# A gated cross-attention layer with a 4-bit FFN: where DVE decodes the weights, and when TensorE turns the FFN's tokens

## The chip, the cores and the metric

One core of one Trainium2 chip. The metric is the device time of one execution in microseconds, the median of the runs. Engines: PE (TensorE), with its weight loads as PEld; DVE (VectorE); ACT (ScalarE); POOL (GpSimd); SP (SyncE), which issues all the DMAs here.

## The reference

Sixteen sequences of 100 tokens, 512 wide. First a cross-attention with 16 heads of 32 onto a context of 361 rows with a mask, then an FFN whose weights are 4-bit codes with a scale for each group of 128:

```
x = x + tanh(g_xattn) * sigmoid(h @ wg.T) * (softmax(q k.T / sqrt(32), masked) v @ wo.T),   h = rmsnorm(layernorm(x)) * norm_w
gate, up = split(layernorm(x) @ dequant(gate_up).T)          # 2 x 1408 rows, 512 wide
y = (silu(gate) * up) @ dequant(down).T                       # 512 rows, 1408 wide
x = x + tanh(g_ffn) * y / sqrt(mean(y * y) + 1e-6)
```

dequant takes a nibble of a 32-bit word, looks it up in a table of 16 values (0 to 6, both signs) and multiplies it by its group's scale.

## The kernel before

Every matrix product in float32 is made of halves: a "hi" half, rounded by ACT, and a "lo" half, the rest, made by DVE (in places by POOL). Three matmuls (hi hi, hi lo, lo hi) make one product.

**Attention.** Four groups of four sequences. A group has 16 steps, one for each head. In step i, PE turns the probabilities of head i (L1364), attends with head i - 1 (L1377), makes the scores of the next four heads in steps 2, 6, 10 and 14 (L1346, L1353), and then does the one to three jobs that BESIDE lists for the step (L271): X (turn normalised tokens, L1315), Q, K, A/B (values), T (turn the heads' outputs), G (gate), O (output product). The jobs share two banks, PJ, in the order of CYCLE (L265), so that a job starts when the low half of the job two before it has been taken out (open_bank, L1287). Q0 also waits for the low half of X3, and each T for its four heads. Steps 11 to 15 already do the jobs of the next group. ACT in a step (L730): pT_hi, the exp of the head two steps ahead, the hi halves of the jobs, ctxT_hi. DVE in a step (L966): pT_lo, attention norm of the head before (reciprocal, o), the row maximum of the head two ahead (nmax), in steps 6 to 9 the statistics of a sequence of the next group, the low halves of the jobs and the outputs, and the normalising of a sequence. Each engine runs its list in order; what is queued behind a wait waits too. POOL makes rstd by a power, ctxT_lo in steps 9 to 11 and the mask bias.

**Decoding beside it.** The FFN's weights are decoded by DVE in the first three of the four groups. A loop body (L1203) goes from step LOOP_FROM = 6 to step 5 of the next group. Each body decodes six pieces, of kinds u, d, u, u, d, u (u: a gate/up tile; d: two down tiles with their scales). A piece goes through stages (decode, L1033): 0 shifts the words (a d piece also cuts its scales), 1 takes the magnitude (d: scale less its cut), 2 puts in the sign, 3 writes `left`, 4 (d alone) writes the second `left`. Piece q lies in step 8 + q, its five stages in five places of the step. SP (L480 to L516) loads the words of pieces 0 and 1 and the first scales at the start of the body (pieces_before), each further piece's when the piece two before it has been decoded, and stores each `left` (512 KB) to DRAM; `words` and `left` have two buffers each. SP's list of a body: pieces 0 to 3, then the loads of the group after (tokens when X has been made, context, mask), pieces 4 and 5, and then the four outputs.

**FFN.** Five groups j of 320 tokens, 11 tiles t of 128 hidden columns each. PE makes eight products into five banks taken in turn (L1526) and two or three chunks of the down product (L1539); ACT and DVE take each product out with its scale (L838, L1221); POOL adds the two halves; then come tanh, two DVE products (L1229 is called gated, L1236) and the halves of the hidden values. The next group's tokens are normalised by DVE in t = 3, 4 and 5 (L1097), turned by PE at the start of t = TURN_AT[m] into bank 1 (transpose_tile, L1410), which waits until mT_lo of the turn before has read that bank; mT_hi is ACT's and mT_lo (L1105) DVE's, at the end of that t.

Of the kernel before, what the change touches and what calls it, by code (L numbers as in the profile page):

```python
# [18 lines left out]
NB = 4  # L19
GROUPS = B // NB  # L20
# [8 lines left out]
STEPS = HEADS  # L29
# [23 lines left out]
KINDS = "uduudu"  # L53
# [7 lines left out]
def build(nc, x, ctx_tail, ctx_full, mask, mask_tail, g_xattn, g_ffn, norm_w, wq, wk, wv, wo, wg,  # L61
          packed, gu_scales, dn_scales, identity, shifts, x1_dram, gu_dram, dn_dram, out):
    es = ExitStack()
    with es:
# [161 lines left out]
        ROUND, TURNED = (2, 3, 4, 5, 0), bank[1]  # L226
        TURN_AT = (5, 6, 7)
        def product_bank(j, t, i, k):
# [52 lines left out]

        PIECE_AT = {8 + q: q for q in range(len(KINDS))}
        STATS_AT, TURNED_AT = 12, {13: 0, 14: 1, 15: 2}
# [67 lines left out]
        def _(sp):  # L351
# [27 lines left out]
            def load_next(g):  # L379

                for b in range(NB):
                    sp.wait_ge(s_pj, split_count(g, f"X{b}"))
                    sp.dma_start(xn[:, b, :], x[bass.ds(NB * (g + 1) + b, 1)].rearrange("o t d -> (o t) d")).then_inc(s_x[b], 16)
# [5 lines left out]
            def outputs(g, last):  # L389
                for b in range(NB):  # L390
                    sp.wait_ge(s_x1, NB * g + b + 1)
                    sp.dma_start(x1_dram[bass.ds(NB * g + b, 1)].rearrange("o t d -> (o t) d"), gate[b][:, :])\
                      .then_inc(s_x1st[b], 16)
                    if b + 2 < NB:
                        load_residual(g, b + 2)
                    elif not last:
                        load_residual(g + 1, b - 2)

# [8 lines left out]

            def keep_piece(g, q):

                for r in range(LEFT[q + 1] - LEFT[q]):  # L410
                    sp.wait_ge(s_left, LEFT[-1] * g + LEFT[q] + r + 1)
                    if KINDS[q] == "u":
                        to = gu_dram[bass.ds(KINDS.count("u") * g + KINDS[:q].count("u"), 1), :, :]
                    else:
                        to = dn_dram[bass.ds(2 * (KINDS.count("d") * g + KINDS[:q].count("d")) + r, 1), :, :]
                    s = (LEFT[q] + r) % 2
                    sp.dma_start(to.rearrange("o p c -> (o p) c"), left[s][:, :].bitcast(F32)).then_inc(s_kept[s], 16)

            def next_piece(g, q):

                if q + 2 < len(KINDS):
                    sp.wait_ge(s_dec, len(KINDS) * g + q + 1)
                    load_piece(g, q + 2)
                keep_piece(g, q)
                if KINDS[q] == "d" and "d" in KINDS[q + 1:]:
                    load_scales(g, KINDS.index("d", q + 1))
# [32 lines left out]
            def full_store(b):  # L459
                sp.wait_ge(f_x1, b + 1)  # L460
                sp.dma_start(x1_dram[bass.ds(b, 1)].rearrange("o t d -> (o t) d"), xa[:, 0, :]).then_inc(f_st, 16)
                sp.wait_ge(f_st, 16 * (b + 1))

            for s in range(2):
                sp.sem_inc(s_kept[s], 16)
            with sp.If(wants_full(sp)):
                sp.wait_ge(s_pjlo, len(HEAD))
                sp.wait_ge(s_mb, 1)
                full_loads(0)
                with sp.Fori(0, B - 1) as b:  # L470
                    full_store(b)
                    full_loads(b + 1)
                full_store(B - 1)
                with sp.Fori(0, GROUPS - 1) as g:
                    pieces_before(g)
                    for q in range(len(KINDS)):
                        next_piece(g, q)
                all_kept()
                phase_barrier(sp)
                load_gate_up(range(FT))  # L480
                load_x1(0)
                load_down()
            with sp.Else():
                for b in range(NB):
                    sp.sem_inc(s_x1st[b], 16)
                for b in range(2):
                    load_residual(0, b)
                load_next(0)
                with sp.Fori(0, GROUPS - 2) as g:
                    pieces_before(g)  # L490
                    for q in range(4):
                        next_piece(g, q)
                    load_next(g + 1)
                    for q in range(4, len(KINDS)):
                        next_piece(g, q)
                    outputs(g, False)
                pieces_before(GROUPS - 2)
                for q in range(len(KINDS)):
                    next_piece(GROUPS - 2, q)
                outputs(GROUPS - 2, False)  # L500
# [12 lines left out]
                load_x1(0)  # L513
                load_down()
                outputs(GROUPS - 1, True)
                for b in range(NB):  # L516
                    sp.wait_ge(s_x1st[b], 16 * (GROUPS + 1))
# [368 lines left out]
        def _(dve):  # L886
# [307 lines left out]
            with dve.Else():  # L1194
# [8 lines left out]
                with dve.Fori(0, GROUPS - 1) as g:  # L1203
                    for i in range(LOOP_FROM, STEPS):
                        step(g, i)
                    for i in range(LOOP_FROM):
                        step(g + 1, i)
                for i in range(LOOP_FROM, STEPS):
# [417 lines left out]
```

## Time and profile before

| | us |
|---|---|
| median of 3 runs (lowest, highest) | 725.06 (722.46, 725.78) |
| profiled execution, its own time | 723.83 |
| its span, first to last instruction | 722.0 |
| PE busy | 601.8 |
| DVE busy | 480.4 |
| ACT busy | 323.3 |
| POOL busy | 227.6 |
| granted clock, mean | 0.898 |

The attention loop's three bodies lie between 69 and 363 us, the FFN between 423 and 722. A granted clock of 1.00 is 2.4 GHz, 0.50 is 1.2 GHz. Busy times overlap, and idle time of an engine costs only where another one waits for it.

### The profile page before, as it was taken

To read this page: it belongs to the slowest core of one execution; us is meant where nothing else is said; L and a number is where in the kernel's file an instruction comes from. 1 tells how busy PE (TensorE), PEld (TensorE's weight loads), DVE (VectorE), ACT (ScalarE), POOL (GpSimd) and SP (SyncE) were. 2 spreads that over 40 slices of the span, in tenths; PEclk is the share of its full clock that TensorE was granted. 3 is DMA by queue.
4 is the path that set the end of the run, shared out by engine and by line. 5 is a ranking of instruction groups with operands and counts; after the bars stand their busy time and mean duration, and the time that the engine had idled before them with its cause. 6 is when DMAs were issued, how large, how long until landed. Compare 5 with 4: busy or idle time off the path is not lost.

```text
span 722.0 us, 12496 instructions
## 1 busy us (share of the span) xinstructions
PE 601.8 (83%) x4154; PEld 528.8 (73%) x4154; DVE 480.4 (67%) x1062; ACT 323.3 (45%) x865; POOL 227.6 (32%) x242
## 2 busy tenths in 40 slices
PE   1699957899858899488997777699699799699997
PEld 1598847888658787488885556587598697599984
DVE  6745795556975569855645349689689679677741
ACT  2754332433325433334343215375465465376630
POOL 5710130000310002100000006487476476477740
PEclk9988976899969999569998599799999999899999
DMA  8440154012451032410286430100100010000011
GB/s 270 144 136 3 46 190 164 1 47 89 156 189 52 24 101 97 160 58 0 68 312 209 180 105 1 65 1 1 65 28 7 26 68 30 30 1 30 30 58 45
DMA packets 26842, 59.36 MB, mean 82 GB/s; under 512 B 3625, under 2 KB 3753, under 8 KB 26793
## 3 DMA queue, kind: packets, MB, share of 16 engines
q1 hardware_dynamic: 26792, 58.76, 24.0%
q8 instruction: 24, 0.39, 0.2%
q14 instruction: 26, 0.20, 0.1%
HBM read 39.62 MB, written 19.14 MB: 81 GB/s over the span
## 4 chain that ended last, share of the span: by engine, by line
PE 50%; DVE 24%; ACT 8%; issue 8%; POOL 7%; DMA 2%; DVEq 0%; SPq 0%; ACTq 0%; POOLq 0%
PE bank L257 19%; PE bank L1526 13%; PE bank L1539 10%; PE bank L1377 3%; ACT probs L719 3%; DVE nmax L937 2%; PE bank L1353 2%; DVE xn L932 2%; POOL hT_lo L629 2%; DVE pT_lo L942 2%; DVE part_gate L1221 1%; DVE vb_lo L905 1%; DVE part_up L1221 1%; DMA xb<-x_scratch 1%; DVE words L1040 1%
## 5 line engine op out<-in xcount | busy, mean ns | idle before, releaser
L1526 PE MATMUL bank<-mT_hi,wgu 128*128 128x320 f32 x440 | 142.2, 333 | 13.9 <-ACT part_up L838 5.4
L1526 PE MATMUL bank<-mT_lo,wgu 128*128 128x320 f32 x440 | 137.9, 323 | 0.0
L719 ACT ACTIVATE probs<-bank,nmax 100x96 f32<-100x96 f32 x256 | 66.1, 342 | 157.3 <-DVE nmax L937 157.3
L1526 PEld LDWEIGHTS bank<-mT_hi,wgu 128*128 128x128 f32 x440 | 88.4, 201 | 25.6 <-ACT part_up L838 7.5
L1526 PEld LDWEIGHTS bank<-mT_lo,wgu 128*128 128x128 f32 x440 | 88.6, 201 | 3.6
L636 POOL TENSOR_TENSOR part_gate<-part_gate 128x320 f32<-128x320 f32 x55 | 57.1, 1039 | 92.8 <-DVE part_gate L1221 92.8
L838 ACT ACTIVATE part_up<-bank,scale 128x320 f32<-128x320 f32 x110 | 57.4, 522 | 56.2 <-PE bank L1526 56.1
L566 POOL TENSOR_TENSOR rstd<-var,halfpow 100x1 f32<-100x1 f32 x16 | 13.7, 857 | 210.4 <-DVE var L927 210.4
L838 ACT ACTIVATE part_gate<-bank,scale 128x320 f32<-128x320 f32 x110 | 52.4, 525 | 61.7 <-PE bank L1526 42.8
L1221 DVE SCALAR_TENSOR_TENSOR part_gate<-bank,scale,part_gate 128x320 f32<-128x320 f32 x110 | 55.8, 545 | 30.1 <-ACT part_gate L838 18.2
L1221 DVE SCALAR_TENSOR_TENSOR part_up<-bank,scale,part_up 128x320 f32<-128x320 f32 x110 | 58.3, 546 | 24.5 <-ACT part_up L838 17.7
L642 POOL TENSOR_TENSOR part_up<-part_up 128x320 f32<-128x320 f32 x55 | 56.9, 1034 | 26.7 <-DVE part_up L1221 25.8
L1539 PE MATMUL bank<-wdn_lo,hT_hi 128*128 128x512 f32 (+1 forms) x143 | 57.3, 401 | 0.0
L1539 PE MATMUL bank<-wdn_hi,hT_hi 128*128 128x512 f32 (+1 forms) x143 | 57.1, 399 | 0.0
L1539 PE MATMUL bank<-wdn_hi,hT_lo 128*128 128x512 f32 (+1 forms) x143 | 56.9, 398 | 0.0
L1377 PE MATMUL bank<-vb_hi,pT_hi 128*100 128x68 f32 x192 | 51.6, 269 | 1.8 <-DVE o L952 1.7
L629 POOL TENSOR_TENSOR hT_lo<-hidden,hT_hi 128x320 fp32r<-128x320 f32 x55 | 49.4, 898 | 9.2 <-ACT hT_hi L852 8.2
L1377 PE MATMUL bank<-vb_lo,pT_hi 128*100 128x68 f32 x192 | 51.6, 269 | 0.0
L1377 PE MATMUL bank<-vb_hi,pT_lo 128*100 128x68 f32 x192 | 51.5, 268 | 0.0
L905 DVE TENSOR_TENSOR vb_lo<-bank,vb_hi 32x256 fp32r<-32x256 f32 (+2 forms) x56 | 23.7, 423 | 39.2 <-ACT vb_hi L699 34.4
L942 DVE TENSOR_TENSOR pT_lo<-bank,pT_hi 128x300 fp32r<-128x300 f32 x64 | 29.9, 466 | 23.6 <-ACT pT_hi L727 22.8
L257 PE MATMUL bank<-xT_hi,wq_hi 128*128 128x400 f32 x64 | 26.8, 418 | 18.3 <-DVE xT_lo L908 17.5
(130 smaller groups left out, 1573.2 us busy)
## 6 DMA issues: line engine op xcount, KB each, us to landing
gate_up_scratch<-left SPq DMA_DIRECT2D x12, 512.0 KB, 5.5
down_scratch<-left SPq DMA_DIRECT2D x12, 512.0 KB, 2.9
wgu<-gate_up_scratch SPq DMA_DIRECT2D x11, 512.0 KB, 7.0
words<-in_packed SPq DMA_DIRECT2D x18, 256.0 KB
xn<-in_x SPq DMA_DIRECT2D x16, 200.0 KB
xa<-in_x SPq DMA_DIRECT2D x16, 200.0 KB
x_scratch<-gate SPq DMA_DIRECT2D x16, 200.0 KB
ctx_raw<-in_ctx_tail SPq DMA_DIRECT2D x4, 768.0 KB, 9.6
```

The source lines that it names most:

```text
L257: last = nc.tensor.matmul(out_ap, lhs(a, t), rhs(b, t), start=t == 0 and p == 0, stop=t == tiles - 1 and p == 2)
L629: nc.gpsimd.tensor_tensor(hT[LO][:, t, cols], hidden[n % 2][:, :], hT[HI][:, t, cols].bitcast(F32), ALU.subtract)\
L636: nc.gpsimd.tensor_tensor(a[:, :], a[:, :], b[:, :], ALU.add).then_inc(s_gate_sum, 1)
L642: nc.gpsimd.tensor_tensor(a[:, :], a[:, :], b[:, :], ALU.add).then_inc(s_up_sum, 1)
L719: last = nc.scalar.activation(probs[i % 2][:, cols], SC[i % HPG][0:L, cols], ACT.Exp, bias=nmax[:, i % 4, b:b + 1])
L838: nc.scalar.activation(part[n % 2][i][k][:, :], product_bank(j, t, i, k)[:, 0:TG], ACT.Copy, scale=scale32[:, t, i, k:k + 1]).then_inc(s_e ...
L905: last = nc.vector.tensor_tensor(value_cols(name, LO, rows, blk), src[rows, 0:HALF].rearrange("p (h d) -> p h d", d=HD), value_cols(name, ...
L942: nc.vector.tensor_tensor(pT[i % 2][LO][:, :, :].rearrange("k c t -> k (c t)"), PT[:, 0:CHUNKS * L], pT[i % 2][HI][:, :, :].rearrange("k c ...
L1221: nc.vector.scalar_tensor_tensor(onto, product_bank(j, t, i, k)[:, 0:TG], scale32[:, t, i, k:k + 1], onto, ALU.mult, ALU.add).then_inc(s_e ...
L1377: last = nc.tensor.matmul(PV[0:L, VW * c:VW * c + 2 * VW].rearrange("t (b w) -> t b w", w=VW), pT[i % 2][ph][:, c, :], vb[vh][:, c, :, VW ...
L1526: last = nc.tensor.matmul(product_bank(j, t, i, k)[:, 0:TG], wgu[t][:, k, 128 * i:128 * i + 128], mT[j % 2][half][:, k, :], start=half == ...
L1539: last = nc.tensor.matmul(bank[6 + slot][0:rows, :], hT[a][:, c, cols], wdn[c][b][:, :], start=c == 0 and p == 0, stop=c == FT - 1 and p == 2)
```

## The change

Three things. The stages of all six pieces are written down as one list of 26 (a u piece has four, a d piece five) and laid two to a step over 13 steps, 6 to 15 and then 0 to 2 of the next group, both at one place of the step: behind the row maximum and ahead of statistics and low halves. SP's list is written step by step in the same order: behind each stage what it allows (a words load, a store, scales), then the step's token loads and outputs; the context's load moves to step 13. In the FFN the three turns go from t = 5, 6, 7 to t = 5, 7, 9, PE's, ACT's and DVE's parts with them.

```diff
-        TURN_AT = (5, 6, 7)
+        TURN_AT = (5, 7, 9)
...
-        PIECE_AT = {8 + q: q for q in range(len(KINDS))}
+        STAGES = [(q, stage) for q in range(len(KINDS)) for stage in range(5 if KINDS[q] == "d" else 4)]
+        DECODE_AT = {((LOOP_FROM + n // 2) % STEPS, 1): STAGES[n:n + 2] for n in range(0, len(STAGES), 2)}
+
+        CONTEXT_AT = 13
...
-            def next_piece(g, q):
-
-                if q + 2 < len(KINDS):
+            def behind_decoding(g, q, stage):
+
+                if stage == 2 and q + 2 < len(KINDS):
                     sp.wait_ge(s_dec, len(KINDS) * g + q + 1)
                     load_piece(g, q + 2)
-                keep_piece(g, q)
-                if KINDS[q] == "d" and "d" in KINDS[q + 1:]:
+                elif stage > 2:
+                    keep(g, q, stage - 3)
+                if stage == 4 and "d" in KINDS[q + 1:]:
                     load_scales(g, KINDS.index("d", q + 1))
...
+            def cycle(g, last=False):
+
+                pieces_before(g)
+                for i in range(LOOP_FROM, LOOP_FROM + STEPS):
+                    i %= STEPS
+                    for place in range(3):
+                        for unit in DECODE_AT.get((i, place), ()):
+                            behind_decoding(g, *unit)
+                    for name in BESIDE[i]:
+                        if name[0] == "X" and not last:
+                            load_tokens(g + 1, int(name[1]))
+                        elif name[0] == "O":
+                            output(g, int(name[1]))
+                    if i == CONTEXT_AT and not last:
+                        load_context(g + 1)
...
                 with sp.Fori(0, GROUPS - 2) as g:
-                    pieces_before(g)
-                    for q in range(4):
-                        next_piece(g, q)
-                    load_next(g + 1)
-                    for q in range(4, len(KINDS)):
-                        next_piece(g, q)
-                    outputs(g, False)
...
+                    cycle(g)
+                cycle(GROUPS - 2, True)
...
-            def step(g, i, last=False):
-                def dequant(stage):
-                    if not last and i in PIECE_AT:
-                        decode(g, PIECE_AT[i], stage)
+            def step(g, i, last=False, cycle=None):
+                def dequant(place):
+                    if cycle is not None:
+                        for q, stage in DECODE_AT.get((i, place), ()):
+                            decode(cycle, q, stage)
 
                 probsT_lo(g, i)
                 dequant(0)
                 if not isinstance(g, int) or g or i:
                     attn_norm(*last_step(g, i))
-                dequant(1)
                 for ahead in step_ahead(g, i):
                     row_max(*ahead)
-                dequant(2)
+                dequant(1)
                 if not last and i in NORM_AT:
                     layer_stats(g + 1, NORM_AT[i])
...
-                dequant(3)
                 for c, name in beside(g, i):
...
-                dequant(4)
+                dequant(2)
```

Every entry of DECODE_AT has place 1, so places 0 and 2 are empty.

## Rows read from the trace of the kernel before

**Rows 1.** The page, busy time of each engine (share of the span) and instructions.
```profile
PE 601.8 (83%) x4154; PEld 528.8 (73%) x4154; DVE 480.4 (67%) x1062; ACT 323.3 (45%) x865; POOL 227.6 (32%) x242
```

**Rows 2.** PE's waits, 69.2 to 363: line waited for, us in total, times, longest.
```profile
PE bank L257 <- DVE xT_lo L908: 16.2, 3, 5.4
```

**Rows 3.** Stretch of step 12: length, busy by engine, granted clock, DMA share, GB/s.
```profile
202.10:215.25 13.15, 7.74 (x38) 7.28 (x37) 8.08 (x15) 2.74 (x8) 2.28 (x2) 0.56 0.71 224
```

**Rows 4.** Timeline of DVE, middle cycle: start, us, instruction, [idle before <-releaser].
```profile
182.29 0.55 DVE L914 TENSOR_TENSOR kT_lo<-bank,kT_hi 128x384 fp32r<-128x384 f32 x1
...
189.59 2.22 DVE L932 TENSOR_SCALAR xn<-xn,mv,rstd 100x512 f32<-100x512 f32 x1
...
207.58 1.05 DVE L908 TENSOR_TENSOR xT_lo<-bank,xT_hi 128x400 fp32r<-128x400 f32 x2
213.62 0.57 DVE L911 SCALAR_TENSOR_TENSOR qT_lo<-bank,qT_hi 128x400 fp32r<-128x400 f32 x1 [5.00 <-ACT qT_hi L705]
```

**Rows 5.** Timeline of PE, middle cycle: T1, G3, Q0 and the scores.
```profile
183.05 0.56 PE L1325 MATMUL bank<-ident,o 100*128 100x100 f32 x4
...
189.73 0.75 PE L257 MATMUL bank<-wg_hi,xT_hi 128*100 128x512 f32 x1 [0.99 <-DVE oT_lo L916]
...
208.68 0.70 PE L257 MATMUL bank<-xT_hi,wq_hi 128*128 128x400 f32 x1 [5.41 <-DVE xT_lo L908]
...
219.49 0.37 PE L1346 MATMUL bank<-mb,ones 1*100 1x384 bf16 x4 [1.63 <-DVE kT_lo L914]
```

**Rows 6.** PE's waits in the FFN, 425 to 700.
```profile
PE bank L1416 <- DVE mT_lo L1105: 24.2, 8, 4.3
```

**Rows 7.** Timeline of PE, FFN group 1, the second turn.
```profile
508.45 0.66 PE L1416 MATMUL bank<-ident,mn 128*128 128x128 f32 x4 [3.15 <-DVE mT_lo L1105]
```

**Rows 8.** DVE's decoding, 69.2 to 363.1: count, busy us, mean ns, idle before.
```profile
L1054 DVE SCALAR_TENSOR_TENSOR fp<-words,fp 128x512 int32<-128x512 int32 x18 | 12.3, 681 | 0.0
...
L1040 DVE TENSOR_SCALAR words<-words,shift 128x512 int32<-128x512 int32 x18 | 9.5, 527 | 0.0
...
L1062 DVE CAST left<-fp 128x1024 fp32r<-128x1024 f16 x12 | 8.3, 694 | 0.7
...
L1047 DVE TENSOR_SCALAR fp<-words 128x512 int32<-128x512 int32 x18 | 8.3, 458 | 0.0
...
L1060 DVE TENSOR_TENSOR left<-fp,scale_a 128x1024 fp32r<-128x1024 f16 x6 | 7.3, 1225 | 0.2
...
L1043 DVE TENSOR_SCALAR scale_a<-scale 128x1024 int16<-128x1024 int16 x6 | 3.4, 570 | 0.0
```

**Rows 9.** Timeline of DVE, step 0 of the middle cycle.
```profile
234.18 0.57 DVE L911 SCALAR_TENSOR_TENSOR qT_lo<-bank,qT_hi 128x400 fp32r<-128x400 f32 x1 [1.50 <-ACT qT_hi L705]
```

**Rows 10.** Timeline of SP, start of the middle cycle: DMA issues.
```profile
168.38 1.39 SPq L400 DMA_DIRECT2D words<-in_packed  x2
```

**Rows 11.** DMA issues of the whole run: count, KB each, median us to landing.
```profile
scale<-in_dn_scales SPq DMA_DIRECT2D x6, 256.0 KB, 6.3
```

**Rows 12.** The same, issued between 263.9 and 269 us.
```profile
scale<-in_dn_scales SPq DMA_DIRECT2D x1, 256.0 KB, 8.3
```

**Rows 13.** Timeline of DVE, FFN groups 0 and 1: gated, and mT_lo at t = 5.
```profile
477.58 0.48 DVE L1229 SCALAR_TENSOR_TENSOR hidden<-tgate,part_gate 128x320 f32<-128x320 f32 x1
480.88 0.48 DVE L1229 SCALAR_TENSOR_TENSOR hidden<-tgate,part_gate 128x320 f32<-128x320 f32 x1
...
507.32 0.47 DVE L1229 SCALAR_TENSOR_TENSOR hidden<-tgate,part_gate 128x320 f32<-128x320 f32 x1
507.71 0.68 DVE L1105 TENSOR_TENSOR mT_lo<-bank,mT_hi 128x512 fp32r<-128x512 f32 x1
...
529.93 0.48 DVE L1229 SCALAR_TENSOR_TENSOR hidden<-tgate,part_gate 128x320 f32<-128x320 f32 x1
533.65 0.48 DVE L1229 SCALAR_TENSOR_TENSOR hidden<-tgate,part_gate 128x320 f32<-128x320 f32 x1
```

More of the change, by code:

```diff
@@ L377, in load_residual, with load_tokens, load_context @@
                 sp.dma_start(xa[:, b % 2, :], x[bass.ds(NB * g + b, 1)].rearrange("o t d -> (o t) d")).then_inc(s_xa[b % 2], 16)
[L379 to L383, printed above, removed]
+            def load_tokens(g, b):
+                sp.wait_ge(s_pj, split_count(g, f"X{b}"))
+                sp.dma_start(xn[:, b, :], x[bass.ds(NB * (g + 1) + b, 1)].rearrange("o t d -> (o t) d")).then_inc(s_x[b], 16)
+            def load_context(g):
                 wait_apart(sp, s_ctxlo, KT * (g + 1))
@@ L387, in load_next, with output @@
                 load_tail_mask(g + 1)
-            def outputs(g, last):
+            def load_next(g):
                 for b in range(NB):
[L391 to L397, printed above, removed]
+                    load_tokens(g, b)
+                load_context(g)
+            def output(g, b, last=False):
+                sp.wait_ge(s_x1, NB * g + b + 1)
+                sp.dma_start(x1_dram[bass.ds(NB * g + b, 1)].rearrange("o t d -> (o t) d"), gate[b][:, :])\
+                  .then_inc(s_x1st[b], 16)
+                if b + 2 < NB:
+                    load_residual(g, b + 2)
+                elif not last:
+                    load_residual(g + 1, b - 2)
             def load_piece(g, q):
@@ L406, in load_scales, with keep @@
                   .then_inc(s_dscale, 16)
[L408 to L417, printed above, removed]
-            def next_piece(g, q):
-                if q + 2 < len(KINDS):
+            def keep(g, q, r):
+                sp.wait_ge(s_left, LEFT[-1] * g + LEFT[q] + r + 1)
+                if KINDS[q] == "u":
+                    to = gu_dram[bass.ds(KINDS.count("u") * g + KINDS[:q].count("u"), 1), :, :]
+                else:
+                    to = dn_dram[bass.ds(2 * (KINDS.count("d") * g + KINDS[:q].count("d")) + r, 1), :, :]
+                s = (LEFT[q] + r) % 2
+                sp.dma_start(to.rearrange("o p c -> (o p) c"), left[s][:, :].bitcast(F32)).then_inc(s_kept[s], 16)
+            def behind_decoding(g, q, stage):
+                if stage == 2 and q + 2 < len(KINDS):
                     sp.wait_ge(s_dec, len(KINDS) * g + q + 1)
                     load_piece(g, q + 2)
-                keep_piece(g, q)
-                if KINDS[q] == "d" and "d" in KINDS[q + 1:]:
+                elif stage > 2:
+                    keep(g, q, stage - 3)
+                if stage == 4 and "d" in KINDS[q + 1:]:
                     load_scales(g, KINDS.index("d", q + 1))
@@ L475, in _ @@
                     pieces_before(g)
-                    for q in range(len(KINDS)):
-                        next_piece(g, q)
+                    for unit in STAGES:
+                        behind_decoding(g, *unit)
                 all_kept()
@@ L489, in _ @@
                 with sp.Fori(0, GROUPS - 2) as g:
-                    pieces_before(g)
-                    for q in range(4):
-                        next_piece(g, q)
-                    load_next(g + 1)
-                    for q in range(4, len(KINDS)):
-                        next_piece(g, q)
-                    outputs(g, False)
[L497 to L500, printed above, removed]
+                    cycle(g)
+                cycle(GROUPS - 2, True)
                 all_kept()
@@ L514, in _ @@
                 load_down()
-                outputs(GROUPS - 1, True)
+                for b in range(NB):
+                    output(GROUPS - 1, b, True)
                 for b in range(NB):
@@ L1204, in _ @@
                     for i in range(LOOP_FROM, STEPS):
-                        step(g, i)
+                        step(g, i, cycle=g)
                     for i in range(LOOP_FROM):
-                        step(g + 1, i)
+                        step(g + 1, i, cycle=g)
                 for i in range(LOOP_FROM, STEPS):
```

## The prediction

> **What bounds the kernel now.** I read the page's busy line first, then who waited for whom on TensorE in the attention loop, the stretches of one cycle, the timelines of DVE and PE at the two worst places, and the same for the FFN. PE is busy 601.8 us of 722.0 [rows 1]: no other engine comes near, so what the kernel can win is PE's idle time and the time at the low clock behind it. Step numbers are those of the code, 0 to 15; a "cycle" is one turn of the attention loop, from step 6 to the next step 5; the middle one runs from 168.9 to 264.9 us.
>
> In the attention loop PE waits longest for DVE's xT_lo, 16.2 us in 3 waits, one of 5.4 us in each cycle [rows 2]. The stretch of step 12 takes 13.15 us with PE busy for 7.74, at a granted clock of 0.56, nearly the 1.2 GHz level throughout [rows 3]. The timelines show why: DVE is busy without a break up to xT_lo at 207.58, among it a whole piece being decoded, then sits idle 5.00 us until the Q0 product has been made [rows 4]. PE stands still for 5.41 us before Q0 at 208.68, 0.99 us before G3 at 189.73 and 1.63 us before the scores at 219.49 [rows 5]. So DVE is late in steps 9 to 13 and idle elsewhere.
>
> In the FFN, PE waits 24.2 us in 8 waits for mT_lo [rows 6]: two in each of the four groups that turn a next one, at t = 6 and t = 7. In group 1 the first is 3.15 us [rows 7], the second much the same. The second and third turn stand one t behind the one before, in PE's program, while the mT_lo that frees the bank comes last in DVE's t.
>
> **The decoding, what it costs.** No instruction is added or taken away: a piece of kind u costs 0.53 + 0.46 + 0.68 + 0.69 = 2.36 us of DVE, one of kind d 0.53 + 0.57 + 0.46 + 0.68 + 0.68 + 2 x 1.22 = 5.36 us [rows 8] (L1054's row stands for L1051 too, L1060's for L1067), four and two of them in a cycle 20.2 us. Before, they lay in steps 8 to 13. Now two stages lie in each of 13 steps (6 to 15, 0 to 2): 0.9 to 2.4 us each, behind the row maximum, so that maximum and attention norm come 1 to 2 us earlier in steps 8 to 13, and exp on ACT with them.
>
> **What it removes, laid out for the middle cycle without a late load.** DVE in step 7 gets 1.35 us and had 0.4 us free, so step 8 starts 1.0 us late; there (1.75 us before the low half, where four stages stood) kT_lo comes at 183.25, 0.96 later than at 182.29 [rows 4]. T1 on PE, which waits for that bank, starts at 183.9 in place of 183.05 [rows 5]. T1 to the end of the scores took 5.7 us, so PE reaches G3 at 189.6. oT_lo is done at 189.3 (maximum at 185.6, two stages of 1.9, statistics 1.25, oT_lo 0.56): no wait. G3 starts only 0.1 us earlier, but at the high clock it takes 2.9 us, as G2 did in step 9, not 4.4, and the turns of probabilities of step 11 start at 192.5. From there, by DVE's durations in order: X0's low half at 197.2, behind pT_hi, the maximum and exp (four of 0.26); X2 at 197.7, X3 at 198.3; pT_hi at 198.1, the maximum at 199.4, exp to 201.05, xT_hi to 201.9, xT_lo of X3 to 202.5. Two stages of 1.2 us fit into DVE's wait. Q0 starts at 202.6 in place of 208.68: 6.1 us gained, and a wait of 3.7 us stays, since exp stands ahead of xT_hi on ACT. I leave Q0 at its slow 4.4 us, the stall ahead of it being still there. In step 13 the maximum, exp and kT_hi come 0.9 us earlier against PE, and the wait of 1.63 us ahead of the scores goes nearly whole: 1.5 us.
>
> **What it adds.** Steps 14, 15, 1 and 2 hide 0.9 to 1.8 us each in waits of DVE for ACT of 1.5 to 3 us. Step 0 doesn't: it gets 1.23 + 1.21 = 2.44 us against an idle 1.50 us ahead of qT_lo [rows 9]; K1 on PE waits for that bank: 0.95 us a cycle lost. So 6.1 + 1.5 - 0.95 = 6.6 us for a cycle.
>
> The larger cost is the load. Piece 0 moves from step 8 to step 6, but SP issues its words as before, behind the last output: at 168.38 [rows 10], when step 6 of DVE starts at 168.87. A load of 256 KB on this queue landed 6.3 us after its issue in the median [rows 11]; the words' own landing is not shown. Bounds: at once (the words then cost nothing, as in the first cycle) and 8.3 us (the scales of the last cycle, issued third behind the two words [rows 12]). I take 6.3, the same size and queue: 174.7. DVE reaches the first stage at 170.2 and stands 4.4 us; queued behind it are the statistics of step 6 and pT_lo of step 7, for which PE's next turn waits. Then 0.9 + 1.25: pT_lo of step 7 at 176.8, not 174.0. Through step 8 the delay is 2.9 us more than above at T1 (186.8), and G3 starts at 192.5, Q0 at 205.6: gain 3.1, and 3.1 + 1.5 - 0.95 = 3.65 us. The first cycle has its words long before. Sum: 6.6 + 2 x 3.7 = 14 us; with the words at once 20, at 8.3 us 10.
>
> The Trainium skill, page "DMA: Bandwidth & Descriptors", section "Anatomy of one DMA — SWDGE (gpsimd) path", has about 2.0 us plus bytes over 436 GB/s for a transfer, an estimate of 2.6 us here; by it DVE would stand 0.8 us and the sum would be near 20 us in place of 14. The trace has 6.3 us, and that is used.
>
> SP's new order: each wait is on something that DVE or PE does in that same step, and every words load is issued two to three steps ahead of its use (some 10 us against 6.3). left's stores get two steps too; the 4 and 8 us for which SP waited between the two stores of a d piece vanish. Nothing. ctx_raw's load goes one step later and is used a cycle on. Nothing.
>
> POOL: the normalising in step 9 took 2.22 us, not 0.54, beside POOL's ctxT_lo [rows 4]. It now comes ahead of ctxT_lo or behind it; between 1.7 us a cycle saved off the path and 1.7 lost I take 0. The skill, page "SBUF — State Buffer", section "Who interferes with whom", says that such an instruction and GpSimd's shut each other out for a whole instruction; with decoding now beside POOL's work of steps 6 to 8 too, that rule would take up to 2 us a cycle off the gain. One row agrees with it.
>
> **The FFN turns.** The turns at t = 7 and 9 find the bank free: mT_lo of the turn before is done at 507.71 + 0.68 = 508.4, and PE gets to t = 7 at 509.4. So all 24.2 us go. What is late next is DVE: it is behind until 507.32 (gated of t = 5) [rows 13], since it normalises in t = 3 to 5. From there it needs 3.30 us a t (two of L1229 in group 0, at 477.58 and 480.88 [rows 13]), 0.68 + 0.68 + 0.42 for three mT_lo and 1.1 for an output tile: 507.32 + 5 x 3.30 + 1.78 + 1.1 = 526.7 for gated of t = 10, which stood at 533.65. PE alone: 505.3 (508.45 less the wait) + 5 x 3.72 (529.93 to 533.65, a t in which PE is the bound [rows 13]) + 1.6 for two turns = 525.5 for the next group's start, which stood at 533.09. DVE's path is the later: 526.2, 6.9 us gained on 6.48 us of waits, since the low clock behind the stalls goes too. Over 24.2 us that is 25.8. Bounds: 17 (DVE at 3.72 a t) and 30 (PE's path alone). I take 25.
>
> **Sum.** 14 + 25 = 39 us off a profiled time of 723.8 (span 722.0 and 1.8 around it): 684.8. The median shown lies 1.2 us higher (725.06): 686.
>
> **Rivals.**
> A: the decoding gains nothing (the words land at 8.3 us or later, collisions with POOL at 1.7 us a step, new waits for low halves). For it: the load's slack is negative. Against: it would have to eat 6.1 us a cycle at Q0. 725 - 25 = 700.
> B: the clock stays up. Step 12 had 0.56 [rows 3]; if Q0 (4.4 against 2.4 us) and the A jobs after it run at 2.4 GHz, 3 us a cycle, and if the words land early, 2 us in two cycles: 686 - 13 = 673. Against: a wait of 3.7 us stays. The skill, "TensorE: Matmul & The Clock Gate", section "What's actually happening", has activity release a throttled clock; the trace agrees, the low clock stands behind the stalls.
> C, slower: every step's pair stands ahead of that step's low halves, which PE needs. If all of the 20.2 us of a cycle came onto PE's path, 61 us in three, against 24 us of waits removed there and 25 in the FFN: 725 + 12 = 737. It decides from 16 us a cycle; the idle times of DVE in 8 of the 13 steps speak against it.
> D: the FFN's waits only move: DVE is the bound there and half stays: 698.
>
> **Chances.** Forecast 0.50 (own range 679 to 694), A 0.15, B 0.20, C 0.03, D 0.10, and 0.02 for no change (a gain in the FFN given back in attention). Below 0.5% (3.6 us) a measurement can't tell. Faster 0.95, same 0.02, slower 0.03. Range 670 to 702: it takes in B at 673, D and A at 700.
>
> **What would show it.** No wait of PE at L1416 for mT_lo in the FFN but up to 1 us; group 1 some 47 us long, not 54. In each cycle the wait ahead of Q0 3.7 us; DVE idle ahead of L1040 in step 6 of the second and third cycle by some 4.4 us and not in the first; K1's wait 1.1 us; cycles of 93, 92 and 94.5 us after 99.7, 96.0 and 98.2. Wrong if these stalls stay while the DVE work has moved, or if the words' wait is above 8 us.

## The result, and the profile after

The changed kernel took 674.87 us (median of 4 runs, 671.74 to 676.95) beside 723.76 for the kernel before on the same chip: ratio 0.932, 95% interval 0.9271 to 0.9369. The forecast was 686 with a range of 670 to 702; the time lies in that range, but below the 679 to 694 that the forecast's own mechanism was given. Run again in another set it took 671.91, ratio 0.9298 (0.9267 to 0.9329).

The profiled execution took 673.74, its span 671.9, 50.1 us less than before. The page's busy line beside [rows 1]:

```profile
PE 581.1 (86%) x4154; PEld 506.1 (75%) x4154; DVE 479.4 (71%) x1062; ACT 323.2 (48%) x865; POOL 223.3 (33%) x242
```

PE runs the same 4154 matmuls in 20.7 us less busy time, at a mean granted clock of 0.937 in place of 0.898: that is clock, not work. The rest of the 50 us is idle time of PE. DVE's busy time is the same to 1 us.

The three cycles of attention, before and then after (length, busy time and count of PE, PEld, DVE, ACT and POOL, granted clock, DMA share, GB/s):

```profile
69.20:168.90 99.70, 85.63 (x708) 75.79 (x700) 66.14 (x151) 37.83 (x118) 9.28 (x9) 0.85 0.26 87
168.90:264.90 96.00, 81.29 (x708) 71.94 (x700) 66.02 (x150) 37.79 (x118) 9.24 (x9) 0.89 0.30 100
264.90:363.10 98.20, 84.18 (x704) 74.82 (x700) 65.98 (x149) 37.75 (x118) 9.25 (x9) 0.86 0.24 80
```

```profile
68.40:158.30 89.90, 81.01 (x700) 71.36 (x692) 65.59 (x149) 37.94 (x118) 7.66 (x9) 0.91 0.30 97
158.30:247.80 89.50, 78.86 (x705) 69.47 (x704) 65.73 (x150) 37.77 (x118) 7.65 (x9) 0.94 0.33 107
247.80:336.70 88.90, 78.89 (x704) 69.50 (x700) 65.67 (x150) 37.70 (x118) 7.66 (x9) 0.94 0.26 89
```

They are 9.8, 6.5 and 9.3 us shorter, 25.6 together. PE's busy time falls by 12.3 us over the three and its idle time by 13.3; the granted clock is 0.85 to 0.89 before and 0.91 to 0.94 after.

Two of the FFN's five groups, j = 1 and j = 3, before and then after:

```profile
479.13:533.09 53.96, 45.43 (x256) 40.54 (x255) 43.61 (x93) 31.56 (x74) 35.26 (x37) 0.97 0.07 23
590.26:645.38 55.12, 46.85 (x255) 41.88 (x254) 43.07 (x93) 31.17 (x73) 33.86 (x36) 0.94 0.06 20
```

```profile
447.92:495.87 47.95, 44.46 (x256) 39.26 (x256) 42.93 (x93) 31.63 (x74) 35.05 (x37) 1.00 0.08 26
547.75:595.28 47.53, 44.29 (x255) 39.18 (x254) 42.50 (x93) 31.14 (x73) 33.68 (x36) 1.00 0.07 23
```

Groups 0 to 3 are 5.1, 6.0, 5.3 and 7.6 us shorter, 24.0 together; the last group, which turns nothing, is 76.62 us in both. So 25.6 + 24.0 = 49.6 of the 50.1 us.

### The profile page after: what moved, and what is told of

Its sections match the earlier page's. It is cut to its first block, busy times and chain, and to the rows that moved or that the text cites. A ratio compares the mean times of both kernels' runs of the same rounds, so it can differ in the third digit from the quotient of the medians.

```text
span 671.9 us, 12496 instructions
## 1 busy us (share of the span) xinstructions
PE 581.1 (86%) x4154; PEld 506.1 (75%) x4154; DVE 479.4 (71%) x1062; ACT 323.2 (48%) x865; POOL 223.3 (33%) x242
## 4 chain that ended last, share of the span: by engine, by line
PE 46%; DVE 25%; ACT 9%; issue 8%; POOL 7%; DMA 3%; SPq 0%; DVEq 0%; ACTq 0%; POOLq 0%
PE bank L257 18%; PE bank L1542 11%; PE bank L1555 10%; ACT probs L736 3%; PE bank L1393 3%; POOL hT_lo L646 2%; DVE part_gate L1237 2%; DVE nmax L954 2%; DVE pT_lo L959 2%; DVE xn L949 2%; DMA words<-in_packed 2%; DVE vb_lo L922 2%; PE bank L1369 2%; POOL part_gate L653 2%; DVE stats L939 1%
## 5 line engine op out<-in xcount | busy, mean ns | idle before, releaser
L1542 PE MATMUL bank<-mT_hi,wgu 128*128 128x320 f32 x440 | 139.9, 328 | 20.0 <-DVE part_up L1237 8.5
L1542 PE MATMUL bank<-mT_lo,wgu 128*128 128x320 f32 x440 | 133.5, 314 | 0.0
L1542 PEld LDWEIGHTS bank<-mT_hi,wgu 128*128 128x128 f32 x440 | 84.4, 192 | 35.5 <-DVE part_up L1237 12.0
L1542 PEld LDWEIGHTS bank<-mT_lo,wgu 128*128 128x128 f32 x440 | 84.7, 193 | 3.3
L583 POOL TENSOR_TENSOR rstd<-var,halfpow 100x1 f32<-100x1 f32 x16 | 9.1, 567 | 206.3 <-DVE var L944 206.3
L954 DVE TENSOR_REDUCE nmax<-bank 100x4 f32<-100x384 f32 x64 | 35.0, 549 | 3.8 <-PE bank L1369 3.8
```

What stands on the lines that cost most here:

```text
L954: nc.vector.tensor_reduce(nmax[:, i % 4, :], SC[i % HPG][0:L, 0:KC].rearrange("t (b k) -> t b k", b=NB), AXIS_X, ALU.max, negate=True).the ...
L1542: last = nc.tensor.matmul(product_bank(j, t, i, k)[:, 0:TG], wgu[t][:, k, 128 * i:128 * i + 128], mT[j % 2][half][:, k, :], start=half == ...
```

## The experiments

Each ratio is against the kernel before on the same chip and in the same set of runs, with the 95% interval, and kernels of different sets are compared by it. The kernel before had medians of 723.76 us (set of the changed kernel), 721.85 (turn_only, decode_only, early_words, piece_a_step), 723.03 (warm, behind_lows, x_hi_first, turn_6_8_10), 722.46 (changed again, all_three, from_step8) and 720.78 (step8_x_warm); the first row has the runs whose profile stands above the prediction. Cycles are the lengths of the three attention cycles in the profiled execution, from the start of one pT_lo of step 6 to the next.

| kernel | us, median | ratio | cycles, us | FFN, us |
|---|---|---|---|---|
| before | 725.06 | 1 | 99.6, 96.0, 98.3 | 298.6 |
| changed | 674.87 | 0.932 (0.9271 to 0.9369) | 89.9, 89.4, 88.9 | 274.6 |
| turn_only | 699.08 | 0.9692 (0.9668 to 0.9716) | 98.1, 96.0, 98.3 | 274.5 |
| decode_only | 699.61 | 0.969 (0.9662 to 0.9719) | 88.0, 92.2, 88.8 | 299.8 |
| early_words | 668.07 | 0.9275 (0.9243 to 0.9308) | 88.0, 87.5, 86.6 | 275.1 |
| piece_a_step | 696.7 | 0.9655 (0.9631 to 0.9679) | 99.2, 96.5, 95.6 | 274.6 |
| warm | 667.68 | 0.9246 (0.9203 to 0.929) | 86.5, 88.4, 88.2 | 274.4 |
| behind_lows | 712.79 | 0.9861 (0.9816 to 0.9906) | 104.9, 102.3, 102.2 | 274.6 |
| x_hi_first | 666.6 | 0.9233 (0.9192 to 0.9275) | 87.1, 85.7, 88.0 | 274.0 |
| turn_6_8_10 | 684.89 | 0.9477 (0.9432 to 0.9523) | 88.1, 89.0, 91.9 | 284.7 |
| changed again | 671.91 | 0.9298 (0.9267 to 0.9329) | 87.9, 91.9, 88.8 | 275.0 |
| all_three | 661.95 | 0.9149 (0.912 to 0.9179) | 86.5, 85.2, 85.3 | 274.3 |
| from_step8 | 663.8 | 0.9185 (0.915 to 0.9221) | 86.7, 85.3, 85.3 | 275.1 |
| step8_x_warm | 668.55 | 0.9273 (0.924 to 0.9307) | 89.1, 86.0, 87.9 | 274.7 |

The changed kernel's own cycles differ by up to 2.8 us between two executions (89.4 and 91.9, 89.9 and 87.9), so a smaller difference of a single cycle tells nothing.

**The two parts apart.** turn_only is the kernel before with one line changed, decode_only the changed kernel with the same line put back:

```diff
-        TURN_AT = (5, 6, 7)
+        TURN_AT = (5, 7, 9)
```

> The kernel before with the FFN turns at t = 5, 7, 9 alone. Theory 1 (the two parts add up and the FFN part is the 24 us of PE waits for mT_lo): 24 to 25 us faster than before, so about 699; no wait of PE for mT_lo in the FFN; the attention loop's three cycles as before, 99.7, 96.0 and 98.2 us. Rival (part of the gain in the FFN comes from attention handing over at another clock or time): less than 20 us.

> The changed kernel with the FFN turns back at t = 5, 6, 7: the decoding's part alone. Theory 1 (the parts add up): 25 us faster than before, about 699; cycles of about 89.5 us; eight waits for mT_lo of 24 us in the FFN. Rival (the attention part was forecast at 14 us and the rest belongs to the FFN): 14 us faster, 710.

Ratios 0.9692 and 0.969, each some 22 to 23 us, 2 to 3 less than their theories 1 gave. Their product, 0.939, lies just outside the changed kernel's interval (up to 0.9369): by the medians the parts make 45 us and the change 49, and where the other 4 are is open. In the profiles they do add up: the FFN has 274 to 275 us with the new turns and 298.6 or 299.8 without, whatever attention does, and the cycles are 268 to 269 us in all with the new decoding and 292.4 or more without. So theory 1 holds in the profiles, and attention's part is 22 us by the medians and 25 by the cycles, where the forecast had 14.

**Spread or place.** piece_a_step keeps the new place and takes the spread away:

```diff
-        DECODE_AT = {((LOOP_FROM + n // 2) % STEPS, 1): STAGES[n:n + 2] for n in range(0, len(STAGES), 2)}
+        DECODE_AT = {(8 + q, 1): [unit for unit in STAGES if unit[0] == q] for q in range(len(KINDS))}
```

> The changed kernel with a whole piece decoded in each of steps 8 to 13, as before, but all of it behind the row maximum and ahead of the low halves. It tells the spreading from the place. Theory 1 (the low halves' lateness is what PE waits for; the spread is what helps): cycles of 96 to 99 us as before, a wait ahead of Q0 of 5 us or more, so 698 to 705. Rival (the earlier row maximum and exp are what helps, since exp stands ahead of xT_hi on ACT): cycles near 91 us, total near 680.

696.7 us, 1.3 us below the range of theory 1 and not told apart from turn_only (0.9655 and 0.9692, the intervals overlap): without the spread the new place alone gains next to nothing. PE's longest waits in its loop (line waited for, us in total, times, longest):

```profile
PE bank L257 <- DVE xT_lo L925: 22.2, 3, 8.1
PE bank L257 <- DVE oT_lo L933: 7.3, 3, 2.6
```

The place is the new one here too, ahead of which the row maximum stands, and the wait for xT_lo grew from 16.2 [rows 2] to 22.2, since a whole piece stood ahead of the low halves. An early maximum alone buys next to nothing; the rival is out.

behind_lows keeps the spread and takes the place away:

```diff
-        DECODE_AT = {((LOOP_FROM + n // 2) % STEPS, 1): STAGES[n:n + 2] for n in range(0, len(STAGES), 2)}
+        DECODE_AT = {((LOOP_FROM + n // 2) % STEPS, 2): STAGES[n:n + 2] for n in range(0, len(STAGES), 2)}
```

> The changed kernel with the two decoding stages of each step behind the low halves and the normalising (place 2) and not ahead of them (place 1). Theory 1 (the pair costs where a low half waits behind it: kT_lo of K3 ahead of T1, qT_lo in step 0): PE's waits ahead of T1 (1.0 us), K1 (0.9 us) and G1 (0.3 us) go, but the pair now stands ahead of the next step's pT_lo, attention norm and row maximum, and steps 11 to 13 get later by some 1 us each: between 2 us less and 4 us more than the changed kernel. Rival (place does not matter, the spread alone does): within 1 us.

A plain miss of both theories: 712.8 us, with cycles of 102 to 105 us, longer than before the change. DVE's timeline at steps 0 and 1 of this kernel's middle cycle:

```profile
234.51 0.47 DVE L959 TENSOR_TENSOR pT_lo<-bank,pT_hi 128x300 fp32r<-128x300 f32 x1
...
237.35 0.57 DVE L928 SCALAR_TENSOR_TENSOR qT_lo<-bank,qT_hi 128x400 fp32r<-128x400 f32 x1 [1.50 <-ACT qT_hi L722]
237.99 0.86 DVE L922 TENSOR_TENSOR vb_lo<-bank,vb_hi 96x256 fp32r<-96x256 f32 x2
238.89 1.23 DVE L1076 TENSOR_TENSOR left<-fp,scale_a 128x1024 fp32r<-128x1024 f16 x1
240.03 1.22 DVE L1083 TENSOR_TENSOR left<-fp,scale 128x1024 fp32r<-128x1024 f16 x1
241.28 0.47 DVE L959 TENSOR_TENSOR pT_lo<-bank,pT_hi 128x300 fp32r<-128x300 f32 x1
...
244.12 0.56 DVE L931 TENSOR_TENSOR kT_lo<-bank,kT_hi 128x384 fp32r<-128x384 f32 x1 [1.48 <-ACT kT_hi L724]
```

DVE still waits 1.50 us for qT_hi and 1.48 for kT_hi, as the kernel before does [rows 9], and then does the pair on top. ACT makes those hi halves behind its exp, and the exp waits for DVE's row maximum; so DVE's idle time lies between its own maximum and its low halves, however late the step starts. Work put there is free up to about that wait; work put at the end of the step delays the next maximum, and the wait comes again behind it. Step 0 to step 1 took 6.8 us here, 4.4 before and 4.9 in the changed kernel. PE's wait for kT_lo ahead of B1 is 4.0 us (1.5 in the changed kernel).

The waits are the smaller part. The three cycles take 41 us more than the changed kernel's, and PE's idle time has 15 of them; the other 26 are busy time of the same matmuls, at a granted clock of 0.80, 0.83 and 0.87 (0.91 to 0.94 in the changed kernel). One stretch of steps 1 and 2, in which the changed kernel's clock is at 1.00:

```profile
242.80:256.50 13.70, 11.77 (x87) 10.15 (x88) 4.21 (x10) 3.89 (x13) 0.00 (x0) 0.50 0.07 27
```

With piece_a_step this says that it takes both, the spread and the place: either alone leaves nothing of attention's gain, or next to nothing.

**The words' wait.** early_words lets SP load the next cycle's words behind the sign stage of pieces 4 and 5:

```diff
-                if stage == 2 and q + 2 < len(KINDS):
+                if stage == 2 and (q + 2 < len(KINDS) or ahead):
...
-                            behind_decoding(g, *unit)
+                            behind_decoding(g, *unit, ahead=not last)
```

(the scales likewise, and pieces_before runs once, ahead of the loop; these lines are left out).

> The changed kernel, but SP loads the words of the next cycle's pieces 0 and 1 as soon as their buffers are free (behind the sign stage of pieces 4 and 5) and the scales behind piece 4's last stage, so that DVE's wait of some 4.1 us in step 6 of the second and third cycle goes. Theory 1 (that wait costs what the forecast's layout gave, 2.9 us a cycle at T1): 5 to 6 us faster than the changed kernel, about 669, PE's wait ahead of T1 gone to 0.1 us or less. Rival (the wait is absorbed by PE's later waits ahead of X2 and Q0, as the first cycle, which had no such wait, took 89.9 us against 89.5 and 88.9): within 2 us of the changed kernel.

668.07 us, ratio 0.9275 beside 0.932 and 0.9298: 2 to 3 us, between the theories, and the intervals overlap. DVE's wait of 4.1 us is gone, PE's wait ahead of T1 falls from 1.0 to 0.3 us, and cycles 2 and 3 are 1.9 and 2.3 us shorter, not 2.9 each. Part is absorbed, but I can't give the share: the first cycle, which had no such wait, moved by 1.9 us too, and is 87.9 us long in the changed kernel's other profile, as here.

from_step8 leaves SP alone and lays the pairs two steps later:

```diff
-        DECODE_AT = {((LOOP_FROM + n // 2) % STEPS, 1): STAGES[n:n + 2] for n in range(0, len(STAGES), 2)}
+        DECODE_AT = {((8 + n // 2) % STEPS, 1): STAGES[n:n + 2] for n in range(0, len(STAGES), 2)}
```

> The changed kernel with the 13 pairs of stages in steps 8 to 15 and 0 to 4, not 6 to 15 and 0 to 2; SP unchanged. Theory 1 (the wait for the words in step 6 goes as it does with the early loads, and steps 3 and 4 have room, DVE waiting there for PE's O product and ACT): 3 to 6 us less than the changed kernel, with the wait ahead of Q0 still 2.8 us. Rival (the pairs with a piece of kind d now meet step 12 and the outputs of steps 2 to 4, whose gated products PE's banks wait for): the same or up to 5 us more.

663.8 us, ratio 0.9185 against 0.9298 in the same set: 8 us less, more than theory 1 gave. Its waits of PE in the loop:

```profile
PE bank L257 <- DVE xT_lo L925: 7.9, 3, 2.6
PE bank L1331 <- DVE xT_lo L925: 5.0, 3, 1.7
PE bank L257 <- DVE kT_lo L931: 4.9, 3, 1.7
...
PE bank L257 <- DVE qT_lo L928: 0.5, 3, 0.2
```

Beside the changed kernel's, the waits ahead of T1 (1.0), G1 (0.3) and K1 (0.9, now 0.2) are gone: step 7 is free of decoding, so kT_lo of step 8 is in time, and the 2.44 us pair that stood in step 0 lies in step 2, where DVE waits for O0's product. The wait for the words is gone too: step 6 of the second cycle takes 5.2 us, 7.8 in the changed kernel of the same set.

**The clock ahead of Q0.** warm puts 8 matmuls whose result is not used into PE's program, into the bank of the turned probabilities, which is free then:

```diff
-                open_bank(c, name)
+                if warm is None:
+                    open_bank(c, name)
...
+                            pe.wait_ge(s_ptlo, warm + 1)
+                            for k in range(WARM):
+                                nc.tensor.matmul(PT[:, 0:GT], W["wk"][HI][:, k % KT, 0:128], W["wk"][HI][:, k % KT, 0:GT],
+                                                 start=True, stop=True)
+                            open_bank(c, name)
                         pe.wait_ge(s_pjlo, split_count(c, "X3"))
```

> The changed kernel, with 8 matmuls of 400 columns put in PE's program ahead of Q0's wait for xT_lo, in a bank that nobody holds then; their result is not used. They fill part of a wait of 2.8 us. Theory 1 (about 11 us of the gain that the forecast had not counted is clock: what PE does ahead of Q0 sets the level at which Q0 and the jobs behind it run): Q0's product takes 2.4 to 3.3 us, not 4.1, the low stretch of 10.3 us in each cycle gets some 3 us shorter, and the total is 2 to 5 us less than the changed kernel's. Rival (the level follows from something else, and the matmuls only stand in the way): no change or 1 to 2 us more.

667.68 us, ratio 0.9246. Q0's product in the stretch from its first matmul to the next turn: before, in the changed kernel, and with these matmuls (columns as above):

```profile
208.68:212.85 4.17, 4.17 (x13) 4.02 (x14) 0.00 (x0) 0.00 (x0) 0.00 (x0) 0.50 0.80 257
```

```profile
194.71:198.62 3.91, 3.91 (x12) 3.84 (x13) 0.00 (x0) 0.00 (x0) 0.00 (x0) 0.54 0.59 209
```

```profile
191.88:194.44 2.56, 2.56 (x13) 2.52 (x13) 0.00 (x0) 0.00 (x0) 0.00 (x0) 0.88 0.68 251
```

The product takes 3.91 us at 0.54 and 2.56 at 0.88, and what differs ahead of it is that PE worked for 3.02 us where it had waited 2.78. PE's granted clock is low for 6.8 us around Q0 in each cycle, and for 10.2 in the changed kernel. So with more matmuls the stretch got shorter: PE's idle time ahead of Q0 is what the edit took away, and the level rose; theory 1 holds for the clock. For the kernel's time it is likely and not shown: the three cycles are 263.1 us in all, 268.2 and 268.6 in the changed kernel's two profiles, but the interval overlaps both of the changed kernel's (0.932 and 0.9298).

**What stands ahead of xT_lo.** x_hi_first adds to early_words: ACT takes X's hi halves ahead of the step's exp, and the pairs of steps 11 and 12 go behind the low halves.

```diff
-        DECODE_AT = {((LOOP_FROM + n // 2) % STEPS, 1): STAGES[n:n + 2] for n in range(0, len(STAGES), 2)}
+        DECODE_AT = {((LOOP_FROM + n // 2) % STEPS, 2 if n // 2 + LOOP_FROM in (11, 12) else 1): STAGES[n:n + 2] for n in range(0, len(STAGES), 2)}
...
                 probsT_hi(g, i)
+                for job in beside(g, i):
+                    if job[1][0] == "X":
+                        job_hi(*job)
                 for ahead in step_ahead(g, i):
                     exp_step(*ahead)
                 for job in beside(g, i):
-                    if job[1][0] != "O":
+                    if job[1][0] not in "OX":
                         job_hi(*job)
```

> The kernel with the early words, and two more edits: ACT takes the hi halves of the X jobs ahead of the exp of the same step, and DVE decodes behind the low halves in steps 11 and 12. Theory 1 (what is left ahead of Q0, 2.8 us, and ahead of X2, 0.9 to 1.6 us, is the row maximum and exp of 1.04 us that stand ahead of xT_hi on ACT): the wait ahead of X2 goes and the one ahead of Q0 falls to 2 us or less; 2 us a cycle, so about 6 us less than with the early words alone. Rival (the later exp makes the next turn of probabilities late instead): within 1 us of it.

The waits are as theory 1 said: none ahead of X2, and ahead of Q0 1.8 us at most in place of 2.8.

```profile
PE bank L257 <- DVE xT_lo L930: 4.8, 3, 1.8
```

The time isn't: 666.6 against 668.1, not told apart. New waits for kT_lo ahead of the scores (0.3 to 0.6 us a cycle) give back a part. The larger part stands in the clock behind them. The first two cycles are 0.9 and 1.8 us shorter than with the early words alone, the third is 1.4 longer, and its steps 13 to 15 take 16.1 us, 13.9 in the other two:

```profile
280.14:296.22 16.08, 15.46 (x146) 15.26 (x145) 11.83 (x30) 7.67 (x24) 0.00 (x0) 0.79 0.20 82
```

The granted clock is 0.79 there and 1.00 in the other two. The wait ahead of the scores is longest in that cycle, 0.62 us, but all three cycles of all_three have one of 1.0 to 1.1 and no such stretch, so what decides it is not shown; only one execution of each kernel is profiled.

**Where the FFN turns stand.** turn_6_8_10 is TURN_AT = (6, 8, 10) in the changed kernel.

> The changed kernel with the FFN turns at t = 6, 8, 10. The waits that came in place of the removed ones are for DVE at t = 6 and 8 (0.8 and 0.6 us in groups 1 and 3), since DVE is late from normalising in t = 3 to 5 and then has mT_lo on top. Theory 1: with no mT_lo at t = 5 DVE has caught up when the first one comes, and each of the four groups gets 0.5 to 1 us shorter: 2 to 4 us less. Rival (the third turn's mT_lo at t = 10 comes so late that the next group's first product waits): 0 to 4 us more.

684.89 us, 10 us slower than the changed kernel by the medians and 11 to 13 by the ratios: the rival, and worse than it said. PE's waits in the FFN, of this kernel and then of the changed one:

```profile
PE bank L1542 <- DVE part_up L1237: 8.8, 14, 1.9
PE bank L1542 <- DVE mT_lo L1121: 6.1, 4, 2.6
...
PE bank L1542 <- DVE part_gate L1237: 4.7, 7, 1.2
```

```profile
PE bank L1542 <- DVE part_up L1237: 8.5, 13, 1.8
...
PE bank L1542 <- DVE part_gate L1237: 2.0, 3, 0.8
```

The first product of a group needs all three mT_lo, and the third of them comes last in DVE's t = 10: 6.1 us of wait come back. The waits for part_up did not fall, so DVE had not caught up either. No wait names mT_lo with the turns at 5, 7, 9; earlier ones (4, 6, 8) were not tried.

**Together.**

> The changed kernel as it is, beside the next two on the same chip, so that they are compared within one set of runs: 673 to 676 us, as before.

> Early words, the X jobs' hi halves ahead of exp with the decoding of steps 11 and 12 behind the low halves, and the 8 matmuls ahead of Q0's wait, all in one. Theory 1 (load wait and clock are separate prices; with x_hi_first the wait ahead of Q0 is 1.5 to 1.8 us, so the matmuls, 1.4 to 3 us of them, stand in the way a little but bring the clock back): 661 to 665, 2 to 5 us less than x_hi_first's 666.6. Rival (the clock is won already by the shorter waits, the matmuls cost their own time): 667 to 670.

> The pairs in steps 8 to 15 and 0 to 4 (SP as in the changed kernel), those of steps 11 and 12 behind the low halves, the X jobs' hi halves ahead of exp on ACT, and the 8 matmuls ahead of Q0's wait. Theory 1 (the words' wait, the wait ahead of X2 and Q0, and the clock are separate prices): from_step8's 663.8 less 1 to 2 us a cycle, 658 to 661, the fastest here. Rival (the pairs of steps 11 and 12, 1.9 and 1.7 us with a d piece, put behind the low halves delay the next row maximum as they do with all pairs there): 663 to 668.

The changed kernel again took 671.91, a little below the 673 to 676 expected. all_three, at 661.95 us and 0.9149, is the fastest kernel run; from_step8 (0.9185), with one expression changed, is close behind, and their intervals overlap. All three of its cycles are 85 to 86.5 us and the wait ahead of Q0 is filled. Piling the same edits onto from_step8 went the rival's way and just past its range: 668.55 us, 5 us slower than from_step8 (6 by the ratios). Two of its waits in the loop:

```profile
PE bank L1342 <- DVE pT_lo L963: 6.4, 3, 2.4
...
PE bank L1373 <- DVE kT_lo L935: 4.6, 3, 1.5
```

The first line is that of the unused matmuls, which may write their bank only behind pT_lo. With two stages of a d piece (1.9 us) behind the low halves of step 11, pT_lo of step 12 is late, and the matmuls, meant to fill a wait, make one. In time that is the smaller part: step 11 takes 0.8 us more than in from_step8 in each cycle, and step 12 0.2 to 0.6 less. The larger part is the clock in steps 13 to 15, behind the second line, the wait of 1.5 us ahead of the scores; here the first cycle:

```profile
108.58:124.67 16.09, 14.55 (x141) 14.34 (x140) 10.98 (x28) 7.70 (x24) 0.00 (x0) 0.79 0.66 193
```

The third is the same; the second, with the same waits, takes 13.88 us at 1.00, as from_step8 does in all three.

## Why the prediction was right, and where its sizes were off

**The FFN part** was forecast at 25 us and measured at 24.0 in the profile. All 24.2 us of waits for mT_lo [rows 6] went. "What is late next is DVE" held: PE's idle time in the FFN fell by 18.2 us, from 43.5 to 25.3, less than the 24.2, as some 6 came back in waits for DVE's part_up (8.5, 4.8 before) and part_gate (2.0, none before); 5.8 us of busy time went with the clock behind the stalls. The group-1 length was given as 47 us and is 47.95. In the FFN the rows held, and the last group's equal 76.62 us is the control. (The bounds 17 and 30 come out at 18 and 28 from the rows that they name; the forecast lies inside either pair.)

**The layout of the middle cycle** held to its scores. From the cycle's first pT_lo, T1 was forecast at 17.9 us (186.8 less 168.87) and came at 17.4; Q0 at 36.7 and came at 36.4. The half microsecond at T1 is a slip of the layout: a pair of 1.75 us stands in step 8 where four stages stood, 2.36 us by the prediction's own sum, so kT_lo should come some 0.4 us late and not 0.96. G3, forecast at 2.9 us at the high clock, took 2.8. T1, Q0 and the scores as in [rows 5], after, with X2 between them (G3, at 181.29, has no wait now):

```profile
175.71 0.56 PE L1341 MATMUL bank<-ident,o 100*128 100x100 f32 x4 [0.98 <-DVE kT_lo L931]
...
190.34 1.59 PE L1331 MATMUL bank<-ident,xn 100*128 100x100 f32 x8 [1.06 <-DVE xT_lo L925]
194.71 0.70 PE L257 MATMUL bank<-xT_hi,wq_hi 128*128 128x400 f32 x1 [2.78 <-DVE xT_lo L925]
203.37 0.37 PE L1362 MATMUL bank<-mb,ones 1*100 1x384 bf16 x4
```

The wait of 0.98 ahead of T1 is the price of two stages in step 7 and of the late words. Ahead of Q0 2.78 us stay (3.7 forecast), and ahead of the scores none of the 1.63.

**The late words** were forecast at 4.4 us of waiting in step 6. DVE, in the changed kernel:

```profile
164.19 0.49 DVE L1056 TENSOR_SCALAR words<-words,shift 128x512 int32<-128x512 int32 x1 [4.11 <-DMA words<-in_packed]
```

4.1 us in the second cycle and none in the first: the two words loads are issued at 157.86 and DVE goes on 6.3 us later, so the median landing of 6.3 us [rows 11] was the right row. The estimate from the Trainium skill, page "DMA: Bandwidth & Descriptors", section "Anatomy of one DMA — SWDGE (gpsimd) path", would have had 0.8 us here; that fit is for DMAs that GpSimd issues, SyncE issues these, and the trace disagrees with it.

**Step 0** was forecast to cost 0.95 us at K1. The wait there is 0.86 us, where it was 0.3 at most before, and over steps 0 to 5 the middle cycle is 0.5 us longer.

**The collision with POOL** was put at nothing between a gain and a loss of 1.7. Normalising in step 9 still takes long:

```profile
180.79 2.42 DVE L949 TENSOR_SCALAR xn<-xn,mv,rstd 100x512 f32<-100x512 f32 x1
```

2.42 us beside 2.22 [rows 4]: nothing, as taken. The rule of the Trainium skill, page "SBUF — State Buffer", section "Who interferes with whom", stays as it was: this row agrees, POOL's ctxT_lo running beside it from 180.95 us on. Of the up to 2 us a cycle that it would take from the gain no row shows any: the decoding instructions of steps 6 to 8 take 0.42 to 0.69 us, as those of step 8 did before.

**The term that was mis-sized** is the attention sum of 14 us, which measured 25.6. By place, over the three cycles: from a cycle's start to step 13 16.0 us were gained (12.3 forecast), in steps 13 to 15 11.1, 7.5 of them busy time (4.5 forecast, the wait ahead of the scores), and in steps 0 to 5 1.6 were lost (2.9 forecast). So the step that counted too little is the one behind Q0: it took the level of the clock there as it stood and counted the scores' wait alone. The stretch from step 13's pT_lo to step 0's, in the first cycle and then in the middle one, before:

```profile
116.98:135.34 18.36, 16.48 (x143) 16.25 (x142) 9.96 (x26) 7.68 (x24) 0.00 (x0) 0.72 0.14 59
...
215.25:231.30 16.05, 13.63 (x144) 13.29 (x143) 9.94 (x26) 7.55 (x24) 0.00 (x0) 0.89 0.16 66
```

and after:

```profile
110.37:124.29 13.92, 13.13 (x151) 12.88 (x151) 11.83 (x31) 7.52 (x24) 0.00 (x0) 1.00 0.43 119
...
199.85:213.70 13.85, 12.98 (x148) 12.67 (x148) 11.83 (x30) 7.50 (x24) 0.00 (x0) 1.00 0.42 117
```

It holds 1.9 us more of DVE's work than before and is 4.4 and 2.2 us shorter; the third cycle is as the first (18.35 us at 0.72, then 13.86 at 1.00). The prediction was laid out for the middle cycle, where this low clock is shortest (3.4 us of it, 10.2 in the first and in the third), and then multiplied. That the idle time gained, 13.3 us, is near the forecast's 14 is chance: the forecast had 1.5 us a cycle of clock in it, at G3, and that came.

Rival B had this mechanism. Its time, 673, is nearer than the forecast's, in part by luck: it holds 4 us for words that land early, and they landed late; 2 us a cycle for Q0, whose product went from 4.17 to 3.91 us; and 1 us a cycle for the A jobs, where steps 13 to 15 lost 3.4, 0.7 and 3.5 us of busy time. The chance of 0.20 was too low: before the change the clock fell at least twice in every cycle, each time behind waits that the same layout took away or shortened. That a wait ahead of the scores always brings the low clock is not shown; all_three has 1.0 to 1.1 us of it in each cycle and no low clock there.

**Rival C** (slower) did not come: it needed more than 16 us a cycle of decoding on PE's path, and the waits of PE that grew are small: over the three cycles those for qT_lo went from 0.8 to 3.3 us, those for vb_lo from 0.8 to 2.4, and 2.2 for kT_lo ahead of T1 are new. A loss from where the decoding stands is real, though, and the place is what kept it off: in behind_lows the cycles are 13 to 15 us longer than in the changed kernel. Rival A is out with decode_only (0.969), D with turn_only (0.9692).

## What to carry to other kernels

Lay filler work where its engine waits, and find that place by the chain that ends the wait: here DVE's wait ran over its own row maximum and ACT's exp, so filler between the maximum and the low halves was nearly free and the same filler at the end of the step cost more than attention's whole gain. Two steps that hand one buffer to and fro across three engines want a free step between them, with slack for what needs the last of them as well. When PE's waits go, count the clock: a stretch that was slow behind a stall can get faster by itself, in every cycle and not only in the one that you lay out, and here it was over a third of the gain (12.3 us in attention and 5.8 in the FFN, of 50.1).

## What had not been expected of the hardware

Eight matmuls with an unused result, 3.02 us of PE's time in a wait, made Q0's product 1.35 us shorter at a granted clock of 0.88 in place of 0.54. Step 12 is 1.9, 1.4 and 0.7 us shorter in the three cycles, 4 us in all, and the kernel's ratio fell by as much or a little more (0.9246 beside 0.9298 and 0.932), though its interval, up to 0.929, overlaps those of both. Decoding put one place later in DVE's list cost attention 41 us, 26 of them longer busy time of the same matmuls at a lower granted clock. A 256 KB load whose 2 KB rows go to 128 partitions kept DVE waiting until 6 us behind its issue, where stores of twice the size landed in 2.8 to 5.5 us by the page's list of issues.
